# A gated two-layer block: feed-forward products kept in PSUM, high parts moved to ScalarE, the down projection one expert behind

## The chip, the cores and the metric

One core of one Trainium2 chip runs the whole program as one launch. The metric is the device time in microseconds; for the kernel before, three runs gave 1088.89, 1092.85 and 1094.4 us, with a median of 1092.85 us.

## The reference, cut to what matters

The input x is 8 sequences of 256 tokens with 256 features (2048 tokens). Two layers follow each other. Each layer adds a cross-attention over 77 context rows, scaled by tanh of a gate, and then adds a feed-forward, scaled by tanh of another gate.

The first feed-forward has 8 experts of width 704, and the expert is chosen by position:

```
x = inputs.reshape(B, E, C, D)           # E = 8, C = 32 tokens of each sequence
gate = einsum('becd,edf->becf', x, w1)
up   = einsum('becd,edf->becf', x, w3)
h    = silu(gate) * up
out  = einsum('becf,efd->becd', h, w2)
```

So each expert sees 8 x 32 = 256 tokens. The second feed-forward has one shared expert of width 1024 for all 2048 tokens, and 7 routed experts of width 1024. Each token goes to its two best routed experts, and each routed expert has 732 slots.

## The kernel before, in words

**Two parts for each number.** All feed-forward products are made from pairs: a high part (the value written in the type fp32r) and a low part (the value less its high part). One product takes three matmuls (`mm3`, L241 to L243): high by high, one high by low, one low by high. The weights come from HBM as fp32 pieces of 128 x 512 (256 KB) into `raw`. ScalarE copies a piece to `w_hi` (`split13` L768 for the gate and up pieces, `split2` L772 for the down pieces), and GpSimd subtracts it to get `w_lo` (L1496).

**First feed-forward** (`first_layer` on each engine, 8 experts). An expert has six gate and up tiles of 128 hidden rows; tile 0 has gate and up rows of the last 64 hidden units side by side, the others have gate in the left half and up in the right half of one PSUM bank of 512. TensorE does 6 matmuls for tile 0 and 12 for each other tile, 66 in all, and then 36 matmuls of the down projection into the two banks `bank_p`. Tile m goes to bank `2 + m % 3`, one of three, so TensorE waits until VectorE has made the product of tile m - 3. ScalarE makes `silu` (L927) and splits the next expert's pieces behind it. VectorE makes the product (L1214) from `silu` and the up half in PSUM into `prod` in SBUF, casts it to `first_hid_hi` (L1218), and subtracts to get `first_hid_lo` (L1222). It also subtracts two of the three down pieces (L1246), since GpSimd has seven others to do. After the sixth tile TensorE goes straight on to the down projection of the same expert, and for each hidden tile it waits for VectorE's low part. Then ScalarE (L940) and VectorE (L1251) each do four scalings of 32 rows out of `bank_p` into `yh`, and these release the next expert's down projection. SyncE (L341 to L349) loads the pieces in one queue, in this order: down piece, gate and up piece, each with a wait for the low part whose place it takes.

**Second feed-forward.** The shared expert runs in four chunks of 512 tokens. Chunk 0 is interleaved with the end of the second attention and with the routing; chunk 1 follows while GpSimd scatters the rows to the slots in HBM with 32 indirect DMAs (L1632). Then come the 7 routed experts, each with two halves of 366 slots and 8 tiles a half (12 matmuls of 366 columns a tile), then six down projections of 122 slots. Chunks 2 and 3 of the shared expert are last, beside 32 indirect gathers on GpSimd (L1647). Here too VectorE does product, cast and subtraction of every tile (`hidden`), ScalarE does silu and the splits, and GpSimd the weights' low part. The first half of a routed expert (8 tiles) carries four down pieces of its own expert; the second half carries the eight gate and up pieces of the next.

**What sets the order.** It is all written by hand: each engine's program is a list, and counting semaphores order them. `gu_psum` says that a tile is in PSUM, `silu_done`, `gu_free` (product made), `hid_hi_done` and `hid_ready` follow it.

Of the kernel before, what the change touches and what calls it, by code (L numbers as in the profile page):

```python
# [48 lines left out]
def flamingo_program(nc, x, ctx_t, attn_w, rows, cols, gates, router_w, w_first, w_second, xe, ye, v_d, out):  # L49
    with ExitStack() as scope:  # L50
# [50 lines left out]
        v_rows = sb("v_rows", [P, 2, D])  # L101
        kb = sb("kb", [P, 2, KT, SC])
        prob_t = sb("prob_t", [P, KT * PT, S])
# [6 lines left out]
        prod = sb("prod", [P, 2, PIECE])  # L110
        first_hid = place[0]
        first_hid_hi = sb("first_hid_hi", [P, M0, S], F32R)
        first_hid_lo = sb("first_hid_lo", [P, M0, S], F32R)
        assert place[0] == first_ffn_end
        place[0] = first_hid
# [91 lines left out]
        y0_psum, y0_done, y0_first = sem("y0_psum"), sem("y0_done"), sem("y0_first")  # L207
# [23 lines left out]
        GU_SHARED = M0 * E0  # L231
# [32 lines left out]
        def _(sp):  # L264
# [85 lines left out]

            for m in range(M0):
                gate_up_load(1, m)
            with sp.Fori(0, E0 - 2) as e:
                for m in range(M0):
                    if m < 3:
                        down_load(e + 1, m)
                    gate_up_load(e + 2, m)
            for j in range(3):
                down_load(E0 - 1, j)

            for m in range(M0):
                sp.wait_ge(lo13, M0 * (E0 - 1) + m + 1)
                sp.dma_start(raw[:, m, :], w_second[0, m]).then_inc(raw_in[m], 16)

# [70 lines left out]
        def _(pe):  # L435
# [180 lines left out]
            def first_layer(e):  # L616

                for m in range(M0):
                    pe.wait_ge(hi13, M0 * e + m + 1)
                    pe.wait_ge(lo13, M0 * e + m + 1)  # L620
                    pe.wait_ge(gu_free, M0 * e + m + 1)
                    for gu in range(1 if m == 0 else 2):
                        for kt in range(KT):
                            c = kt * (P if m == 0 else 2 * P) + gu * P
                            rhs = [a[:, kt, :].rearrange("p (b s) -> p b s", s=S)[:, :, bass.ds(e * C0, C0)] for a in (act_hi, act_lo)]
                            last = mm3(banks[2 + m % 3][:, gu * S:(gu + 1) * S], w_hi[:, m, c:c + P], w_lo[:, m, c:c + P],
                                       rhs[0], rhs[1], kt == 0, kt == KT - 1)
                    last.then_inc(gu_psum, 1)
                pe.wait_ge(y0_done, 2 * e + 2)
                for k in range(M0):  # L630
                    j, c = k // 2, k % 2 * D
                    pe.wait_ge(hid_ready, hid_count(M0 * e + k))
# [6 lines left out]
                    for h in range(HALVES):  # L639
                        last = mm3(bank_p[h][:, 0:D], first_hid_hi[:, k, h * P:(h + 1) * P], first_hid_lo[:, k, h * P:(h + 1) * P],  # L640
                                   w_hi[:, M0 + j, c:c + D], w_lo[:, M0 + j, c:c + D], k == 0, k == M0 - 1)
                last.then_inc(y0_psum, 1)

# [88 lines left out]
            with pe.Fori(0, E0) as e:  # L732
                first_layer(e)
# [30 lines left out]
        def _(act):  # L764
# [164 lines left out]
            def first_layer(e, i, part):  # L929

                for m in range(M0):
                    src = banks[2 + m % 3]
                    silu_of(M0 * e + m, m % 2, src[0:64, 0:S] if m == 0 else src[:, 0:S], 64 if m == 0 else P, S)
                    if m < 3:
                        split2(M0 + m, e + 1, M0 + m)
                    split13(m, e + 2, m)

                act.wait_ge(y0_psum, e + 1)
                for j in range(B // HALVES):
                    last = nc.scalar.activation(  # L940
                        yh[i * C0:(i + 1) * C0, j, bass.ds(part * D, D)], bank_p[0][j * C0:(j + 1) * C0, 0:D],
# [777 lines left out]
```

## Time and profile before

| what | value |
|---|---|
| median of three runs | 1092.85 us (1088.89 to 1094.4) |
| profiled execution, first to last instruction (the span) | 1084.2 us |
| its own whole time | not given apart from the three runs; the median lies 8.65 us above the span |
| TensorE matmul busy | 927.4 us (86%) |
| VectorE busy | 768.7 us (71%) |
| GpSimd busy | 517.0 us (48%) |
| ScalarE busy | 368.4 us (34%) |

The profile names the engines PE (TensorE matmul), PEld (its weight load), DVE (VectorE), ACT (ScalarE), POOL (GpSimd) and SP (SyncE). A number such as L1222 is the line of the kernel. PEclk is the granted clock of TensorE as a share of full speed. Matmuls are pipelined, so a matmul's own duration is longer than the distance from its start to the next start; the distance is what it costs. Work outside the span is what the launch adds before the first instruction and behind the last.

### The profile page before, as it was taken

The numbers are of one execution on the slowest core, as the hardware profiler recorded it, in microseconds if no ns is written. First come the engines' busy times: TensorE is split into PE (matmuls) and PEld (weight loads), VectorE is DVE, ScalarE is ACT, GpSimd is POOL, SyncE is SP. The second block draws the span as 40 slices with busy tenths as digits, with TensorE's granted clock in tenths as the row PEclk, the third lists the DMA queues.
The fourth block names the chain that finished last, engine by engine and source line by source line (L and its number), as shares of the span: only waits on it lengthen the run. The fifth ranks groups of instructions, "written<-read, shape, count | busy, mean of one in ns | idle before, by whom it ended". The sixth has DMA issues, their size and how long they took to land.

```text
span 1084.2 us, 17578 instructions
## 1 busy us (share of the span) xinstructions
PE 927.4 (86%) x5464; PEld 815.0 (75%) x5464; DVE 768.7 (71%) x1375; ACT 368.4 (34%) x773; POOL 517.0 (48%) x479
## 2 busy tenths in 40 slices
PE   5888887787876879888773999999999999999758
PEld 3666666787874657666562789999999999998637
DVE  4899995978785899998731666758494949475237
ACT  2454453454442444445210232323241414132001
POOL 5667664646362866664567223223142424131740
PEclk9999999988886999999996899999999999999859
DMA  5321112443431000001211232314141413040321
GB/s 181 123 66 38 61 32 85 129 132 126 135 116 31 16 11 10 10 12 43 78 64 59 65 102 65 122 57 135 40 141 36 135 42 129 21 124 29 93 82 59
DMA packets 74860, 82.27 MB, mean 76 GB/s; under 512 B 33902, under 2 KB 47666, under 8 KB 74692
## 3 DMA queue, kind: packets, MB, share of 16 engines
q1 hardware_dynamic: 71748, 74.30, 22.0%
q0 software_dynamic: 3072, 7.46, 2.3%
q8 instruction: 21, 0.34, 0.1%
q14 instruction: 19, 0.16, 0.0%
HBM read 64.57 MB, written 18.10 MB: 76 GB/s over the span
## 4 chain that ended last, share of the span: by engine, by line
PE 47%; DVE 24%; issue 15%; another core or an unknown queue 4%; ACT 4%; POOL 3%; DMA 2%; DVEq 1%; ACTq 0%; SPq 0%; POOLq 0%
PE score L241 9%; PE score L242 8%; PE score L243 8%; PE bank_p L241 5%; DVE total L1084 5%; PE bank_p L243 5%; PE bank_p L242 5%; DVE xn L1039 4%; DVE mx L1075 4%; DVE stats L1014 2%; DVE prob L1079 2%; DMA raw<-w_second_d 2%; DVE prod L1214 1%; PE bank L496 1%
## 5 line engine op out<-in xcount | busy, mean ns | idle before, releaser
L1496 POOL TENSOR_TENSOR w_lo<-raw,w_hi 128x512 fp32r<-128x512 f32 x158 | 211.5, 1350 | 342.8 <-ACT w_hi L772 223.1
L927 ACT ACTIVATE silu<-score 128x366 f32<-128x366 f32 (+3 forms) x192 | 90.8, 473 | 426.3 <-PE score L243 315.8
L1214 DVE TENSOR_TENSOR prod<-silu,score 128x366 f32<-128x366 f32 (+3 forms) x192 | 101.1, 527 | 81.3 <-ACT silu L927 65.3
L241 PE MATMUL score<-xe_hi,w_hi 128*128 128x366 f32 x448 | 149.6, 334 | 2.3 <-DVE prod L1214 2.0
L242 PE MATMUL score<-xe_lo,w_hi 128*128 128x366 f32 x448 | 148.4, 331 | 0.0
L243 PE MATMUL score<-xe_hi,w_lo 128*128 128x366 f32 x448 | 147.1, 328 | 0.0
L241 PE MATMUL score<-act_hi,w_hi 128*128 (+1 forms) x304 | 109.0, 358 | 35.4 <-issue 22.9
L241 PE MATMUL bank_p<-w_hi,hid_hi 128*122 128x256 f32 (+1 forms) x464 | 131.6, 284 | 4.0 <-issue 2.0
L243 PE MATMUL bank_p<-w_hi,hid_lo 128*122 128x256 f32 (+1 forms) x464 | 130.4, 281 | 2.3 <-issue 2.3
L242 PE MATMUL bank_p<-w_lo,hid_hi 128*122 128x256 f32 (+1 forms) x464 | 130.3, 281 | 1.2 <-issue 1.2
L1486 POOL TENSOR_TENSOR prob<-prob,recip 128x616 f32<-128x616 f32 x64 | 96.6, 1511 | 66.0 <-DVE recip L1086 65.9
L1218 DVE CAST hid_hi<-prod 128x366 fp32r<-128x366 f32 (+1 forms) x144 | 116.0, 806 | 5.0
L243 PE MATMUL score<-act_hi,w_lo 128*128 (+1 forms) x304 | 105.5, 347 | 4.2 <-issue 4.1
L242 PE MATMUL score<-act_lo,w_hi 128*128 (+1 forms) x304 | 106.4, 350 | 2.7 <-issue 2.5
L241 PEld LDWEIGHTS score<-act_hi,w_hi 128*128 128x128 f32 x304 | 62.2, 205 | 47.7 <-issue 30.3
L241 PEld LDWEIGHTS score<-xe_hi,w_hi 128*128 128x128 f32 x448 | 84.4, 188 | 6.3 <-DVE prod L1214 4.8
L241 PEld LDWEIGHTS bank_p<-w_hi,hid_hi 128*122 128x122 f32 (+1 forms) x464 | 85.5, 184 | 4.7 <-DVE hid_lo L1222 1.9
L243 PEld LDWEIGHTS bank_p<-w_hi,hid_lo 128*122 128x122 f32 (+1 forms) x464 | 85.9, 185 | 3.9 <-issue 3.9
L807 ACT ACTIVATE prob<-prob 128x616 f32<-128x616 f32 x64 | 46.0, 718 | 123.1 <-DVE prob L1079 123.0
L1222 DVE TENSOR_TENSOR hid_lo<-prod,hid_hi 128x366 fp32r<-128x366 f32 (+1 forms) x136 | 84.2, 619 | 4.7
L477 PE MATMUL score<-kb,q_t 128*128 (+2 forms) x256 | 84.0, 454 | 3.2 <-ACT q_t L801 2.9
L242 PEld LDWEIGHTS bank_p<-w_lo,hid_hi 128*122 128x122 f32 (+1 forms) x464 | 85.7, 185 | 1.0 <-issue 0.8
(141 smaller groups left out, 1941.6 us busy)
## 6 DMA issues: line engine op xcount, KB each, us to landing
raw<-w_second_d SPq DMA_DIRECT2D x108, 256.0 KB, 5.8
raw<-w_first_d SPq DMA_DIRECT2D x72, 256.0 KB, 3.1
slots_in<-yh SPq DMA_DIRECT2D x8, 640.5 KB, 3.1
yh<-slots_in SPq DMA_DIRECT2D x7, 732.0 KB
slots_out<-yh SPq DMA_DIRECT2D x7, 732.0 KB
v_blk<-values SPq DMA_DIRECT2D x256, 5.0 KB, 1.9
wa<-attn_w_d SPq DMA_DIRECT2D x8, 256.0 KB, 5.1
residual<-x_d SPq DMA_DIRECT2D x1, 1792.0 KB, 9.7
```

The costliest lines, as they stand in the source:

```text
L241: nc.tensor.matmul(o, a_hi, b_hi, start=start, stop=False)
L242: nc.tensor.matmul(o, a_hi, b_lo, start=False, stop=False)
L243: return nc.tensor.matmul(o, a_lo, b_hi, start=False, stop=stop)
L477: last = nc.tensor.matmul(score[u % 2][:, c:c + w], q_t[:, dt, qt * P:(qt + 1) * P], kb[:, b % 2, dt, c:c + w], start=True, stop=True)
L807: nc.scalar.activation(pv, pv, ACT.Exp).then_inc(exp_done, 1)
L927: nc.scalar.activation(silu[0:rows_n, buf, 0:width], src, ACT.Silu).then_inc(silu_done, 1)
L1084: nc.vector.tensor_reduce(total[:, u], of_heads(prob[u]), AX_X, ALU.add).then_inc(sum_done, 1)
L1214: nc.vector.tensor_tensor(prod[0:rows_n, buf, 0:width], silu[0:rows_n, buf, 0:width], up, ALU.mult).then_inc(gu_free, 1)
L1218: nc.vector.tensor_copy(hi, prod[0:rows_n, buf, 0:hi.shape[-1]]).then_inc(hid_hi_done, 1)
L1222: nc.vector.tensor_tensor(lo, prod[0:rows_n, buf, 0:hi.shape[-1]], hi.bitcast(F32), ALU.subtract).then_inc(hid_ready, 1)
L1486: nc.gpsimd.tensor_tensor(by_row(prob[u]), by_row(prob[u]), recip[:, u].unsqueeze(1).to_broadcast([P, KV, HT]), ALU.mult).then_inc(norm_do ...
L1496: return nc.gpsimd.tensor_tensor(w_lo[:, at, :], raw[:, slot_f, :], w_hi[:, at, :].bitcast(F32), ALU.subtract)
```

## The change

- **First feed-forward, hidden tiles.** Each of the six tiles has its own PSUM bank (0 to 5). VectorE writes the product over the up half in PSUM. ScalarE copies it from there to the high part, and VectorE subtracts the high part from the product in PSUM to get the low part.
- **First feed-forward, order.** High and low parts have two buffers (even and odd experts), and the down weights too. TensorE does the gate and up tiles 0 and 1 of expert e, then the down projection of expert e - 1, then tiles 2 to 5 of expert e. After the last expert its own down projection follows.
- **First feed-forward, outputs.** ScalarE and VectorE each scale one bank of 128 rows at once into `y0_rows`, and SyncE moves them to `yh` with four DMAs for an expert. The last expert's outputs go as before. The loops of ScalarE and VectorE are partly written out.
- **Routed experts and shared chunks 1 to 3.** ScalarE makes the high part of the hidden tile, one tile behind its silu. VectorE makes the product of tile f and then the low part of tile f - 1, and it also makes the weights' low parts, which leave GpSimd's list.

```diff
             def first_gate_up(e, m):
+                pe.wait_ge(hi13, M0 * e + m + 1)
+                pe.wait_ge(lo13, M0 * e + m + 1)
+                pe.wait_ge(hid0_ready, M0 * e + m + 1)
...
+                            last = mm3(banks[m][:, gu * S:(gu + 1) * S], w_hi[:, m, c:c + P], w_lo[:, m, c:c + P],
+            def first_down(e, par):
+                pe.wait_ge(y0_kept, 2 * e + 2)
...
+                    pe.wait_ge(hid0_ready, M0 * (e + 1) + k + 1)
...
+            def first_layer(e, par, before_it):
+                for m in range(M0):
+                    first_gate_up(e, m)
+                    if m == 1 and before_it:
+                        first_down(e - 1, 1 - par)
# ScalarE
+                for m in range(M0):
+                    first_silu(e, m)
+                    if m > 0:
+                        first_high(e, par, m - 1)
                     if m < 3:
+                        split2(M0 + m, e + 1, M0 + 3 * par + m)
                     split13(m, e + 2, m)
+                    if m == 1 and before_it:
+                        act.wait_ge(y0_psum, e)
...
+                        nc.scalar.activation(y0_rows[:, 1 - par, 0, :], bank_p[0][:, 0:D], ACT.Identity,
+                                             scale=tanh_gate[:, 2:3]).then_inc(y0_kept, 1)
+                first_high(e, par, M0 - 1)
# VectorE
+                nc.vector.tensor_tensor(up, silu0[0:rows_n, m % 4, :], up, ALU.mult).then_inc(prod0_done, 1)
...
+                nc.vector.tensor_tensor(hid0_lo[par][0:rows_n, m, :], up, hid0_hi[par][0:rows_n, m, :].bitcast(F32),
+                                        ALU.subtract).then_inc(hid0_ready, 1)
# SyncE
+            def place_outputs(e):
+                part, i = divmod(e, P // C0)
+                sp.wait_ge(y0_kept, 2 * e + 4)
+                for j in range(P // C0):
+                    sp.dma_start(yh[i * C0:(i + 1) * C0, j::P // C0, part * D:(part + 1) * D],
+                                 y0_rows[j * C0:(j + 1) * C0, e % 2, :, :]).then_inc(y0_moved, 16)
...
                 for m in range(M0):
                     if m < 3:
                         down_load(e + 1, m)
                     gate_up_load(e + 2, m)
+                    if m == 3 and e > 0:
+                        place_outputs(e - 1)
# routed experts, ScalarE
+                        silu_of(n, f % 2, banks[2 + 2 * (f % 2)][:, 0:HC], P, HC)
+                        if hf > 0 or f > 0:
+                            g = (f - 1) % FT
+                            hidden_high(n - 1, g, HC * (hf if f > 0 else 0), HC)
# routed experts, VectorE
-                        hidden(GU_ROUTED + 2 * FT * e + FT * hf + f, f % 2, banks[2 + 2 * (f % 2) + 1][:, 0:HC], P, hf * HC, f, HC)
+                        product(n, f % 2, banks[2 + 2 * (f % 2) + 1][:, 0:HC], P, HC)
+                        if hf > 0 or f > 0:
+                            g, at = (f - 1) % FT, HC * (hf if f > 0 else 0)
+                            hidden_low(n - 1, g % 2, P, hid_hi[:, g, at:at + HC], hid_lo[:, g, at:at + HC])
+                            routed_low(e, hf if f > 0 else 0, g)
# routed experts, GpSimd
-            for f in range(FT):
-                low13(PIECES0 + FT + f, f, f)
-            with pool.Fori(0, E1) as e:
-                expert(e)
-            for j in range(4):
-                low2(3 * E0 + 4 * (STREAM - 1) + j, j, FT + j)
```

## Rows read from the trace of the kernel before

**Rows 1.** Busy time by stage: us, then PE, PEld, DVE, ACT, POOL, PEclk, DMA share.

```profile
184.00:332.00 148.00, 119.49 (x820) 114.80 (x820) 115.13 (x190) 67.38 (x150) 79.26 (x58) 0.86 0.39 121
545.00:597.00 52.00, 27.19 (x148) 23.19 (x148) 11.33 (x28) 6.05 (x9) 36.94 (x36) 0.77 0.18 65
627.00:985.00 358.00, 355.75 (x2428) 351.30 (x2428) 240.44 (x404) 106.43 (x222) 110.20 (x84) 1.00 0.27 87
```

**Rows 2.** Waits, 184 to 332 us: who waited for whom, us, times, longest.

```profile
PE bank_p L241 <- DVE first_hid_lo L1222: 27.8, 16, 2.5
SPq L349 <- DVE w_lo L1246: 45.1, 14, 5.6
```

**Rows 3.** TensorE in order of time: start, duration, [idle before].

```profile
193.67 0.28 PE L241 MATMUL bank_p<-w_hi,first_hid_hi 128*128 128x256 f32 x1
...
228.65 0.29 PE L241 MATMUL bank_p<-w_hi,first_hid_hi 128*128 128x256 f32 x1
...
229.96 0.28 PE L243 MATMUL bank_p<-w_hi,first_hid_lo 128*128 128x256 f32 x1
232.30 0.38 PE L241 MATMUL bank_p<-w_hi,first_hid_hi 128*128 128x256 f32 x1 [2.07 <-DVE first_hid_lo L1222]
...
331.20 0.59 PE L519 MATMUL bank<-wa,ctx_b 128*77 128x256 f32 x2
```

**Rows 4.** Groups by shape, 184 to 332 us: busy us, mean ns, idle before.

```profile
L1496 POOL TENSOR_TENSOR w_lo<-raw,w_hi 128x512 fp32r<-128x512 f32 x56 | 78.0, 1420 | 62.9 <-ACT w_hi L772 59.2 <-ACT w_hi L768 3.6
L1218 DVE CAST first_hid_hi<-prod 128x256 fp32r<-128x256 f32 x40 | 28.8, 720 | 0.0
L1222 DVE TENSOR_TENSOR first_hid_lo<-prod,first_hid_hi 128x256 fp32r<-128x256 f32 x40 | 28.8, 720 | 0.3
L1246 DVE TENSOR_TENSOR w_lo<-raw,w_hi 128x512 fp32r<-128x512 f32 x16 | 27.2, 1698 | 0.0
L1214 DVE TENSOR_TENSOR prod<-silu,score 128x256 f32<-128x256 f32 x40 | 16.4, 409 | 6.4 <-ACT silu L927 6.4
L927 ACT ACTIVATE silu<-score 128x256 f32<-128x256 f32 x40 | 15.1, 376 | 24.7 <-DVE prod L1214 22.7 <-PE score L243 2.0
L768 ACT ACTIVATE w_hi<-raw 128x512 fp32r<-128x512 f32 x48 | 30.0, 624 | 0.0
L1251 DVE TENSOR_SCALAR yh<-bank_p,tanh_gate 32x256 f32 x29 | 13.9, 480 | 20.8 <-PE bank_p L243 20.5
```

**Rows 5.** VectorE in order of time: one operation twice in one expert.

```profile
230.92 1.15 DVE L1222 TENSOR_TENSOR first_hid_lo<-prod,first_hid_hi 128x256 fp32r<-128x256 f32 x1
...
234.22 0.41 DVE L1222 TENSOR_TENSOR first_hid_lo<-prod,first_hid_hi 128x256 fp32r<-128x256 f32 x1
```

**Rows 6.** DMA, 184 to 332 us: GB/s in 40 slices of 3.7 us; issues with KB and us to landing.

```profile
GB/s 0 88 56 143 255 103 144 19 189 275 13 141 3 182 295 19 142 24 153 308 11 139 11 154 315 19 100 42 157 297 42 71 11 103 302 337 27 0 14 149
...
raw<-w_first_d SPq DMA_DIRECT2D x57, 256.0 KB, 2.7
```

**Rows 7.** Groups by shape, 627 to 985 us (routed experts).

```profile
L1218 DVE CAST hid_hi<-prod 128x366 fp32r<-128x366 f32 x112 | 91.8, 820 | 3.9
L1222 DVE TENSOR_TENSOR hid_lo<-prod,hid_hi 128x366 fp32r<-128x366 f32 x112 | 66.6, 595 | 3.9
L1214 DVE TENSOR_TENSOR prod<-silu,score 128x366 f32<-128x366 f32 x112 | 59.5, 531 | 28.7 <-ACT silu L927 28.4
L927 ACT ACTIVATE silu<-score 128x366 f32<-128x366 f32 x112 | 53.5, 478 | 231.7 <-PE score L243 231.7
```

**Rows 8.** ScalarE in order of time, routed experts: one silu to the next.

```profile
641.66 0.48 ACT L927 ACTIVATE silu<-score 128x366 f32<-128x366 f32 x1 [1.54 <-PE score L243]
643.68 0.48 ACT L927 ACTIVATE silu<-score 128x366 f32<-128x366 f32 x1 [1.54 <-PE score L243]
```

**Rows 9.** VectorE, 569 to 571 us (128 x 512, GpSimd on indirect DMAs).

```profile
570.21 0.69 DVE L1222 TENSOR_TENSOR hid_lo<-prod,hid_hi 128x512 fp32r<-128x512 f32 x1
```

**Rows 10.** Waits of the whole trace.

```profile
ACT silu L927 <- remote: 87.6, 4, 41.7
```

More of the change, by code:

```diff
@@ L984, in _ @@
             act.wait_ge(zero_out, 16 * B)
-            per = E0 // HALVES
-            with act.Fori(0, HALVES) as part:
-                for i in range(per):
-                    first_layer(per * part + i, i, part)
+            first_layer(0, 0, False)
+            first_layer(1, 1, True)
+            first_layer(2, 0, True)
+            with act.Fori(1, E0 // 2 - 1) as pair:
+                first_layer(2 * pair + 1, 1, True)
+                first_layer(2 * pair + 2, 0, True)
+            first_layer(E0 - 1, 1, True)
+            last_outputs()
             attention(1)
@@ L1238, in first_layer @@
-                    src = banks[2 + m % 3]
-                    product(n, buf, src[64:P, 0:S] if m == 0 else src[:, S:2 * S], rows_n, S)
+                    first_product(e, m)
                     if m > 0:
-                        hidden_low(*tile(m - 1), first_hid_lo[0:64 if m == 1 else P, m - 1, :])
-                    hidden_high(n, buf, rows_n, hi)
+                        first_low(e, par, m - 1)
+                    if m == 1 and before_it:
+                        dve.wait_ge(y0_psum, e)
+                        if not (isinstance(e, int) and e < 3):
+                            dve.wait_ge(y0_moved, 64 * (e - 2))
+                        nc.vector.tensor_scalar(y0_rows[:, 1 - par, 1, :], bank_p[1][:, 0:D], tanh_gate[:, 2:3], None,
+                                                ALU.mult).then_inc(y0_kept, 1)
@@ L1377, in _ @@
             dve.wait_ge(k_psum, 2)
[L1378 removed]
+            for t in hid0_hi + hid0_lo:
                 last = nc.vector.memset(t[64:P, 0, :].bitcast(F32), 0.0)
@@ L1384, in _ @@
             dve.sem_inc(hid_ready, HID_FREE)
-            dve.sem_inc(y0_done, 2)
-            per = E0 // HALVES
-            with dve.Fori(0, HALVES) as part:
-                for i in range(per):
-                    first_layer(per * part + i, i, part)
+            dve.sem_inc(prod0_done, 4)
+            dve.sem_inc(hid0_ready, M0)
+            dve.sem_inc(y0_kept, 2)
+            first_layer(0, 0, False)
+            first_layer(1, 1, True)
+            first_layer(2, 0, True)
+            with dve.Fori(1, E0 // 2 - 1) as pair:
+                first_layer(2 * pair + 1, 1, True)
+                first_layer(2 * pair + 2, 0, True)
+            first_layer(E0 - 1, 1, True)
+            last_outputs()
             attention(1)
```

174 lines of the change are left out of this document (109 added, 65 removed).

## The prediction, as it was put on record before the changed kernel ran

> **What bounds the kernel now.** I read the table of busy time by stage first. In the routed experts (627 to 985 us) TensorE's matmuls are busy 355.75 of 358.00 us at a granted clock of 1.00: nothing but fewer matmuls helps there. In the first feed-forward (184 to 332 us) they are busy 119.49 of 148.00 us at a clock of 0.86, VectorE 115.13 us and GpSimd 79.26 us [rows 1]. So this stage has room, and the waits say what ends last in it: TensorE's down projection waited 27.8 us in 16 waits for VectorE's low part of the hidden tile [rows 2]. In order of time, the down projection runs the first 12 matmuls at once (two hidden tiles) and then stands still until 232.30, 2.07 us, for a low part [rows 3].
>
> The rest of the stage's loss is the clock. Of the 12 matmuls ahead of that stop the first starts at 228.65 and the last at 229.96, so at full clock they are 1.31 / 11 = 0.119 us apart. From 193.67, the first down projection, to 331.20, when the stage has ended, TensorE issues 8 x 36 + 7 x 66 = 750 matmuls in 137.5 us, 0.183 us each [rows 3]. The waits explain some 28 us, or 0.037 of the 0.064 us more; most of the rest is matmuls behind the waits at a clock below full (mean 0.86 [rows 1], so a mix of 2.4 and 1.2 GHz). Both go if TensorE never waits.
>
> Why VectorE is late: product 0.409, cast 0.720 and low part 0.720 us a tile, six times, and 1.698 us twice for the down weights [rows 4], 14.5 us an expert with the outputs. The cast and the low part are not slow in themselves. The low part takes 1.15 us while GpSimd works and 0.41 us in the same expert when it doesn't [rows 5]. The product, which reads one operand from PSUM, has a mean of 0.409 us [rows 4] beside the same GpSimd.
>
> **The change part by part: first feed-forward.** TensorE's work stays 102 matmuls an expert, 102 x 0.119 = 12.1 us at full clock [rows 3]. The question is whether the others fit below 12.1 us and whether anything is due earlier than they deliver it.
>
> VectorE: six products at 0.41, six low parts, two down weights at 1.70 [rows 4], one output of 128 x 256 at 0.48 (the row of the 32 x 256 output, same columns [rows 4]). The new low part reads the product in PSUM and the high part in SBUF, the same sources as the product: I take 0.41. The upper bound is the low part beside GpSimd, 1.15 us [rows 5]. The product now writes to PSUM, which no row shows; below it can hardly be under the 0.41 of now, above I bound it by the same 1.15. Sum: 2.5 + 2.5 + 3.4 + 0.5 = 8.9 us; with slow low parts 13.3 us; with both slow 17.7 us.
>
> The Trainium skill (SBUF — State Buffer, "SBUF: two separate sides") says that VectorE and GpSimd share one port pair as an exclusive lock, which a VectorE instruction takes when it has two SBUF inputs (against a GpSimd operation that reads SBUF) or runs in a two-port mode. By that rule the low part with its PSUM input never takes the lock and the sum is 8.9 us; the two down weights keep it. The trace agrees as far as it goes: 1.15 against 0.41 us for two SBUF inputs, 0.409 on average for one.
>
> ScalarE: six silus at 0.376, six high parts (bounded by 0.376 below, by the 0.624 of a 128 x 512 copy above; I take 0.376), nine splits at 0.624 and one output at 0.48 [rows 4]: 10.6 us, 12.1 us at the upper bound. It is in order and now waits at tile 1 for the down projection of the expert before. TensorE's order gives 0.7 us for tile 0, 1.4 for tile 1, then 4.2 for the down projection: at 6.3 us ScalarE is released, and silu 2 is due at 7.8. From there it has to do tiles 2 to 5 and then tiles 0 and 1 of the next expert before the next release at 18.4: six silus, six high parts, nine splits, 10.1 us, due at 17.9. It fits by 0.5 us. If it doesn't, what is late is a scaling of `bank_p`, and that is not due for TensorE before the next down projection, a whole turn of slack less its own 6 us. VectorE behind the same release needs 8.9 of its 10.6 us.
>
> GpSimd: seven weights at 1.42 us [rows 4], 9.9 of 12.1 us. Its lows are for the next expert. Tile 5's is split at about 13 us and subtracted by 15 us; TensorE wants it at 22.
>
> Down projection, now 2.1 us of gate and up work later: the last low part follows the end of tile 5 by silu 0.38, product 0.41, a split that stands in ScalarE's queue 0.62, high 0.38, low 0.41, 2.2 us. TensorE is at hidden tile 5 of the down projection only 2.1 + 5 x 0.7 = 5.6 us after the end of tile 5. The wait for a free bank, too, is an expert old with six banks. So nothing is late next, and I expect the 16 waits to be gone.
>
> SyncE and the DMAs: the pieces are 9 x 256 KB and the moved outputs 4 x 64 KB, 2.6 MB an expert, 217 GB/s at 12.1 us. The stage's slices reach 308 and 337 GB/s for 3.7 us [rows 6], and a piece lands in 2.7 us [rows 6], while each load has most of a turn before its split. SyncE's queue now waits 45.1 us for VectorE's down weights [rows 2], and the gate and up loads stand behind it; in the new order these come at 10 and 12 us of the turn and the splits that need the loads behind them at 21 us and later. The four moves an expert stand behind the load of tile 3, and their own condition is older than that load's. I cost them at nothing; if the transfers ran at the 120 to 180 GB/s that surround the peaks [rows 6] the stage would be theirs (see the rivals).
>
> Sum: the first 66 matmuls stay as they are, to 193.67. Then 750 x 0.119 = 89.3 us instead of 137.5: 48.2 us less. I give back 1.5 us for the first turns of longer loops and the last down projection, whose last low parts are due at 3.5 us and come at 2.2 to 3. That leaves 46.7 us. The end of the stage (the last outputs in eight scalings) is as before.
>
> **Routed experts and shared chunks.** A tile is 2.02 us of TensorE (silu to silu, 641.66 to 643.68 [rows 8]). VectorE in the second half: product 0.53, low part 0.54 to 0.60 [rows 7], gate and up weights 0.69 by the row of the same shape with two SBUF inputs [rows 9], together 1.8 us; before it was 0.53 + 0.82 + 0.60 [rows 7]. The upper bound for the weights' low part is 1.70 [rows 4], a row beside a working GpSimd; here GpSimd is idle, so I take 0.69. ScalarE: silu 0.48, high part at most 0.62, split 0.62: 1.7 us. The product of tile f stands behind the low parts of tile f - 1 but TensorE wants it only before tile f + 2. Everything stays below 2.02 us, and as TensorE is never idle now, the gain is 0. In the chunks TensorE sets the pace too. Where the down projection waits for hidden tiles, the new chain is at most 1 us shorter or longer. The two stretches with indirect DMAs hold 87.6 us in which ScalarE's silu waits for a signal that the profile can't attribute, the longest 41.7 us [rows 10]; during the scatter TensorE is busy 27.19 of 52.00 us [rows 1]. The transfers and the work in these stretches stay, so I cost them at 0.
>
> The span comes to 1084.2 - 46.7 = 1037.5 us, and the median, 8.65 us above the span for the kernel before, to 1046.2 us.
>
> **The rivals.**
> - *VectorE stays the bound in the first feed-forward* (0.10). The low part, or the product written to PSUM, takes longer than 0.41. At 13.3 us an expert and with waits that pull the clock down, 14 us: 8 x 14 = 112 us instead of 100 us (9.3 + 89.3 + 1.5), 1058 us. Against it is the mean of 0.409 beside a busy GpSimd.
> - *The transfers become the bound* (0.05). At 180 GB/s an expert takes 14.5 us, 8 x 14.5 = 116 us: 1062 us. Against it: the pauses between the peaks are SyncE's waits, not slow packets [rows 2, 6].
> - *The indirect stretches change* (0.08). Signals from TensorE come late there, for a reason that I can't see. With other neighbours in time, fewer may be late: up to 25 us of TensorE's 52.00 - 27.19 us idle could go, 1020 us. The other direction, 10 us more, is 1055 us.
> - *The routed experts become VectorE's: slower than before* (0.04). The place is the second half, tile by tile. The gain is used up when each of 8 x 7 = 56 tiles costs 46.7 / 56 = 0.83 us more, that is at 2.85 us of VectorE a tile. With weights at 1.70 and a low part at 1.15 a tile is 0.53 + 1.15 + 1.70 = 3.4 us, 1.36 us over TensorE's 2.02: 56 x 1.36 = 76 us, 1122 us. For it: such durations are in the trace. Against it: only beside a working GpSimd, and GpSimd has left this stage.
> - *It doesn't do what it says* (0.03). A wait that I missed ties the down projection to its own expert again, for instance ScalarE's stop at tile 1 delaying the splits; about half the gain is left, 1070 us.
>
> **How the numbers follow.** The forecast has 0.70, with its own range of 1039 to 1055 us (the product or low part up to 0.2 us more at no cost, ScalarE's 0.5 us of margin gone at up to 1 us an expert). The predicted time is 1046 us. The range that leaves out no more than 0.2 goes from 1034 to 1064 us: it leaves out the slower case, the half gain and most of the indirect gain. 0.5% of 1092.85 is 5.5 us, about what a measurement of this kernel can tell from no change. Faster by more: 0.92; within it: 0.03; slower by more: 0.05.
>
> **What would show it.** The down projection's waits for low parts gone, matmul starts 0.119 us apart and PEclk near 1.00 through the stage, its length 99 to 102 us. VectorE's low part and product at 0.41 us beside a working GpSimd; the down weights still at 1.7. The routed stage at 358 us, VectorE's weights at 0.69. The prediction is wrong if the stage is over 107 us, if the routed stage grows by more than 5 us, or if the stretches of indirect DMAs change by more than 5 us.

## The result, and the profile after

Four runs each on one chip: 1040.87 us median (1039.39 to 1041.57) after, 1090.87 us median (1086.1 to 1094.4) before; the ratio is 0.9546, 95% interval 0.952 to 0.9572. The prediction was 1046 us. The profiled execution of the changed kernel has a span of 1037.6 us; the sum of the prediction was 1037.5 us.

The sections between six points in the two traces. All but the last, the end of the span, are starts of TensorE instructions: the first gate and up matmul of the first feed-forward, the first matmul of the second attention (the last row of [rows 3]), the second matmul of the position sums of the routing, the first matmul on slots, and the first matmul of shared chunk 2.

```
                      start   first FF  attention 2  scatter  routed   tail     span
before                184.3     146.9      214.6       81.1    357.6    99.7   1084.2
after                 188.5     100.3      213.4       79.4    353.0   103.0   1037.6
difference             +4.2     -46.5       -1.2       -1.7     -4.6    +3.3    -46.5
predicted                0      -46.7          0          0        0       0    -46.7
```

Busy time of the changed kernel in the first feed-forward, in the middle of it, and in the routed experts, in the columns of [rows 1]: length, PE, PEld, DVE, ACT, POOL, PEclk, DMA share, GB/s.

```profile
188.00:289.00 101.00, 97.58 (x817) 97.43 (x818) 55.36 (x126) 73.23 (x180) 75.07 (x58) 1.00 0.65 196
200.00:284.00 84.00, 84.00 (x707) 84.00 (x706) 45.35 (x104) 59.95 (x150) 63.34 (x49) 1.00 0.67 206
582.00:934.00 352.00, 351.39 (x2419) 350.74 (x2418) 189.44 (x375) 150.71 (x334) 0.00 (x0) 1.00 0.28 89
```

Against the first line of [rows 1], TensorE is busy 97.58 of 101.00 us at a clock of 1.00, where it was 119.49 of 148.00 at 0.86. Its busy time fell too, though it does the same matmuls: they no longer run partly at half clock. VectorE is down from 115.13 to 55.36 us. Between 192 and 286 us the list of waits has no row for TensorE at all, so the first row of [rows 2] is gone. The second is still there and only shorter, 31.6 us where it was 45.1, and TensorE waits for nothing behind it:

```profile
SPq L357 <- DVE w_lo L1348: 31.6, 14, 4.4
```

TensorE in order of time. The first matmul below is the 67th of the stage, the last but one is the 816th:

```profile
196.39 0.28 PE L249 MATMUL bank<-act_hi,w_hi 128*128 x1
...
285.69 0.28 PE L251 MATMUL bank_p<-w_hi,hid_lo_odd 128*128 128x256 f32 x1
288.86 0.41 PE L539 MATMUL bank<-wa,ctx_b 128*77 128x256 f32 x1 [2.89 <-DMA ctx_b<-ctx_d]
```

From 196.39 to 285.69 is 89.3 us for the 750 matmuls that took 137.5 us before [rows 3]. Then TensorE stands 2.89 us for a load of the second attention.

VectorE and ScalarE by shape in the stage: busy us, mean ns, idle before.

```profile
L1322 DVE TENSOR_TENSOR score<-silu,score 128x256 f32<-128x256 f32 x32 | 13.6, 425 | 13.7 <-ACT silu L969 13.7
L1348 DVE TENSOR_TENSOR w_lo<-raw,w_hi 128x512 fp32r<-128x512 f32 x16 | 13.5, 841 | 0.0
L1329 DVE TENSOR_TENSOR hid_lo_odd<-score,hid_hi_odd 128x256 fp32r<-128x256 f32 x16 | 6.7, 418 | 1.2 <-ACT hid_hi_odd L975 1.2
L1342 DVE TENSOR_SCALAR y_rows<-bank_p,tanh_gate 128x256 f32<-128x256 f32 x7 | 3.4, 484 | 15.4 <-PE bank_p L251 10.1 <-DMA yh<-y_rows 5.3
...
L802 ACT ACTIVATE w_hi<-raw 128x512 fp32r<-128x512 f32 x48 | 30.5, 635 | 3.9 <-DMA raw<-w_second_d 3.9
L975 ACT ACTIVATE hid_hi_odd<-score 128x256 fp32r<-128x256 f32 x16 | 6.2, 390 | 0.0
```

The low part, 0.720 us in the mean before [rows 4], takes 0.418 us; the product written to PSUM takes 0.425 us; the down weights' low part fell from 1.698 [rows 4] to 0.841 us, though nothing was done to it. VectorE now waits for ScalarE's silu, that is, for work to arrive.

### The profile page after: what moved, and what is told of

Read it like the earlier page. It is cut to its first block, busy times and chain, and to the rows that moved or that the text cites. A ratio compares the mean times of both kernels' runs of the same rounds, so it can differ in the third digit from the quotient of the medians.

```text
span 1037.6 us, 17237 instructions
## 1 busy us (share of the span) xinstructions
PE 905.1 (87%) x5464; PEld 803.0 (77%) x5464; DVE 642.2 (62%) x1268; ACT 428.9 (41%) x936; POOL 387.0 (37%) x383
## 4 chain that ended last, share of the span: by engine, by line
PE 58%; DVE 23%; issue 11%; POOL 3%; ACT 2%; DMA 2%; DVEq 1%; SPq 0%; POOLq 0%; ACTq 0%
PE score L249 11%; PE score L250 11%; PE score L251 10%; PE bank_p L249 6%; PE bank_p L251 6%; PE bank_p L250 6%; DVE total L1161 5%; DVE xn L1116 5%; DVE mx L1152 4%; DVE stats L1091 2%; DVE prob L1156 2%; DMA raw<-w_second_d 1%; PE score L471 1%; PE bank L516 1%; PE bank L532 1%
## 5 line engine op out<-in xcount | busy, mean ns | idle before, releaser
L961 ACT ACTIVATE silu<-score 128x366 f32<-128x366 f32 (+1 forms) x144 | 72.6, 504 | 342.4 <-PE score L251 296.8
L1292 DVE TENSOR_TENSOR prod<-silu,score 128x366 f32<-128x366 f32 (+1 forms) x144 | 82.0, 569 | 141.7 <-ACT silu L961 132.1
L1759 POOL DMA_INDIRECT act_hi<-slots_out,slot_get x8 | 8.1, 1007 | 406.9 <-DMA slots_out<-yh 404.8
L249 PE MATMUL score<-act_hi,w_hi 128*128 128x512 f32 (+2 forms) x256 | 90.1, 352 | 27.7 <-issue 26.5
L249 PEld LDWEIGHTS bank_p<-w_hi,hid_hi 128*122 128x122 f32 (+1 forms) x464 | 86.5, 186 | 16.8 <-issue 14.3
L1620 POOL TENSOR_TENSOR w_lo<-raw,w_hi 128x512 fp32r<-128x512 f32 x62 | 82.1, 1357 | 22.7 <-ACT w_hi L802 20.9
L250 PE MATMUL score<-act_lo,w_hi 128*128 128x512 f32 (+2 forms) x256 | 88.8, 347 | 0.0
L251 PE MATMUL score<-act_hi,w_lo 128*128 128x512 f32 (+2 forms) x256 | 88.6, 346 | 0.0
L250 PEld LDWEIGHTS score<-xe_lo,w_hi 128*128 128x128 f32 x448 | 84.4, 188 | 0.0
L251 PEld LDWEIGHTS score<-xe_hi,w_lo 128*128 128x128 f32 x448 | 84.2, 188 | 0.0
```

Of the source, the lines that this page charges most:

```text
L249: nc.tensor.matmul(o, a_hi, b_hi, start=start, stop=False)
L250: nc.tensor.matmul(o, a_hi, b_lo, start=False, stop=False)
L251: return nc.tensor.matmul(o, a_lo, b_hi, start=False, stop=stop)
L961: nc.scalar.activation(silu[0:rows_n, buf, 0:width], src, ACT.Silu).then_inc(silu_done, 1)
L1292: nc.vector.tensor_tensor(prod[0:rows_n, buf, 0:width], silu[0:rows_n, buf, 0:width], up, ALU.mult).then_inc(gu_free, 1)
L1620: return nc.gpsimd.tensor_tensor(w_lo[:, at, :], raw[:, slot_f, :], w_hi[:, at, :].bitcast(F32), ALU.subtract)
```

## The experiments

There were twelve runs of eleven kernels, each beside the kernel before on the same chip. They ran on four chips, and on two of these the kernel before takes 1055.5 and 1056.8 us, not 1090. The first feed-forward doesn't differ between the chips: with the changed kernel's code in it, it took 100.1, 100.3 and 103.8 us on the slower ones and 101.1 and 101.2 us on the others (the stretches at fault come below). So for it I compare stage lengths, which are in each trace, and the time of a turn: from one expert's down projection to the next, a mean over the first six turns. The turn is the sharper measure. It was 12.16 us in all five of these runs, while their first matmul came anywhere from 185.5 to 188.5 us and the length moved with it, so a difference of less than 4 us in the length says little.

```
kernel                 turn    first FF   median     before on    ratio [95% interval]
                       us      us         us         that chip
kernel before          18.1    146.9
old_work_no_defer      16.5    136.7      1043.03    1055.49      0.9876 [0.9845, 0.9907]
old_tile_work          15.3    126.3      1069.88    1089.81      0.9806 [0.9779, 0.9833]
psum_only              14.3    112.9      1021.43    1056.84      0.9678 [0.9651, 0.9706]
no_defer               12.1    102.1      1041.87    1089.81      0.9551 [0.9519, 0.9583]
high_dve               12.2    101.6      1003.21    1055.49      0.9513 [0.9482, 0.9544]
prod_sbuf              12.2    100.9      1012.61    1055.49      0.9587 [0.9549, 0.9626]
changed kernel         12.2    100.3      1040.87    1090.87      0.9546 [0.952, 0.9572]
old_tile_short_pool    12.2    100.1      1003.89    1056.84      0.951 [0.9476, 0.9545]
```

The last row has two executions, and its kernel leaves out part of the work (below).

**Which half of the change is it? First the first feed-forward alone.** Routed experts and chunks as before:

```diff
-                            hidden_high(n - 1, g, HC * (hf if f > 0 else 0), HC)   # ScalarE
+                        hidden_high(n, f % 2, P, hid_hi[:, f, hf * HC:(hf + 1) * HC])   # VectorE
+            with pool.Fori(0, E1) as e:
+                expert(e)   # the weights' low parts on GpSimd
```

> The new first feed-forward with the routed experts and shared chunks as before (VectorE makes product, high and low part, GpSimd the weights' low parts). Theory: nearly the whole gain is the first feed-forward's. The two traces give -49.7 us for that stage and +4.2 us ahead of it, and the routed stage gives -4.6 us by itself; so this kernel should stand 4 to 6 us above the changed one, a span of 1042 to 1044 us, with the routed stage back at 357.6 us. Rival: the 4.6 us of the routed stage are a matter of where code and data came to lie, not of who makes the high part; then the span is within 1.5 us of 1037.6.

1044.6 us (1043.01 to 1048.05) against 1089.81, ratio 0.9587 [0.9557, 0.9617]; span 1041.3 us. That is 3.7 us above the changed kernel, just short of the theory's 4 to 6 and far from the rival's 1.5, but the 3.7 us don't lie where the theory put them: the routed stage is 356.0 us (3.0 more than changed), not 357.6, the scatter stretch 82.7 us (3.3 more), and the tail 100.4 us (2.5 less). The -49.7 us of the expectation count the first feed-forward to its last down projection, without the 3.2 us behind it.

**Then the routed part alone.** The reverse edit on the kernel before.

> The first feed-forward as before, the routed experts and shared chunks as changed. Theory: 4.6 us less than the kernel before in the routed stage (357.6 to 353.0 us) and nothing elsewhere, a span of 1079 to 1081 us. Rival one: the routed part gains nothing by itself (my prediction, 0), a span of 1084. Rival two: the 3.2 us more that the changed kernel's tail takes (99.8 to 102.9 us from the third shared chunk to the end) come from this part; then this kernel shows them as well and is near 1083 us.

1087.9 us (ten runs) against 1089.81, ratio 0.9979 [0.9957, 1.0001]; span 1085.4 us. Routed stage 353.1 us, 4.5 less than before, as the theory said; tail 103.1 us, 3.4 more, as the second rival said. In all the routed part gives 1.9 us by the medians, and the interval reaches 1, so by itself it can't be told from nothing. The span is 4 us over the theory's 1079 to 1081 us. Its trace shows one more thing: it reaches the first feed-forward at 187.5 us with the same code for which the profiled run of before needed 184.3, 3.2 us less.

**Is the delay of the down projection needed?**

```diff
                 for m in range(M0):
                     first_gate_up(e, m)
-                    if m == 1 and before_it:
-                        first_down(e - 1, 1 - par)
+                first_down(e, par)
```

> The changed kernel with one thing undone, on TensorE alone: the down projection of expert e stands right behind its own tile 5 again, not behind tile 1 of the next expert. Theory by the prediction's steps: the low part of tile 5 is ready 2.2 to 3 us after the tile, TensorE wants it at 3.5 us, so the delay by one expert is not what removes the waits; 0 to 2 us more in the stage. Rival: the low part comes after 3.5 us, TensorE stops once an expert for 1 to 2 us, and the clock falls with it: 10 to 20 us more.

1041.87 us median on a chip where before took 1089.81, and a span of 1037.1 us; a turn is 12.1 us. Its four executions took 1038.9, 1040.66, 1043.08 and 2703.28 us. The median is that of all four, the ratio leaves the last one out, and why it took so long is open. It isn't needed: with the new tile work the low part of tile 5 is there when TensorE asks for it, and the trace has no wait of TensorE for it. The 1.8 us more in the stage lie ahead of its first down projection and behind its last, not in its turns.

**Is it the order, or the work on the tile?** The changed order, banks and outputs, with the tile work of before:

```diff
-                nc.vector.tensor_tensor(up, silu0[0:rows_n, m % 4, :], up, ALU.mult).then_inc(prod0_done, 1)
+                nc.vector.tensor_tensor(prod0[0:rows_n, m % 4, :], silu0[0:rows_n, m % 4, :], up, ALU.mult).then_inc(prod0_done, 1)
+                nc.vector.tensor_copy(hid0_hi[par][0:rows_n, m, :], prod0[0:rows_n, m % 4, :]).then_inc(hid0_high, 1)
```

> The changed order, banks and output moves, but the tile work as before: VectorE makes product into SBUF, high and low part from SBUF. Theory: VectorE's work sets the stage, 6 x (0.41 + 0.72 + 0.72) + 2 x 1.70 + 0.5 = 15.0 us an expert against TensorE's 12.1; the stage is 17 to 25 us longer than with the changed tile work, a span of 1055 to 1063 us. Rival: the order alone (the down projection an expert behind) removes the waits and VectorE's durations shrink when nothing waits; then less than 5 us more.

The stage took 126.3 us, 26 more than changed, just over the expected 17 to 25, and the span 1067.7 us, over the expected 1055 to 1063; the whole took 1069.88 us in the median, ratio 0.9806. VectorE sets the pace. By shape, from 187 to 314 us:

```profile
L1337 DVE TENSOR_TENSOR hid_lo_even<-prod,hid_hi_even 128x256 fp32r<-128x256 f32 x20 | 20.4, 1018 | 0.1
L1357 DVE TENSOR_TENSOR w_lo<-raw,w_hi 128x512 fp32r<-128x512 f32 x16 | 19.6, 1228 | 0.0
L1330 DVE CAST hid_hi_odd<-prod 128x256 fp32r<-128x256 f32 x20 | 14.3, 717 | 0.0
```

The low part takes 1.0 us. And the waits of TensorE and the stretch in the middle of the stage, with the columns as above:

```profile
PE bank_p L250 <- DVE hid_lo_odd L1337: 10.0, 8, 2.6
PE bank_p L250 <- DVE hid_lo_even L1337: 6.3, 7, 1.6
...
200.00:305.00 105.00, 92.11 (x706) 89.22 (x704) 92.64 (x145) 51.59 (x112) 69.19 (x48) 0.95 0.53 165
```

VectorE is busy 92.64 of 105 us, 13.5 us of a turn of 15.3, and TensorE waits twice an expert for its low part (15 waits).

**The same without the delay.** Both edits together:

> The tile work of before on VectorE (product into SBUF, high and low part from SBUF) and the down projection right behind its own tile 5; what is left of the change in the first feed-forward is a bank for each of the six tiles, two buffers for the hidden parts and the down weights, and the outputs scaled 128 rows at once and moved by DMA. Theory: with VectorE as the bound, the delay by one expert does matter: TensorE stops for the last low parts and VectorE then for TensorE; 8 to 14 us longer than the 126.3 us with the delay. Rival: VectorE alone sets the pace in both orders, within 3 us of 126.3; then the banks and the outputs alone are the 20 us between 126.3 and the 146.9 us of before.

136.7 us, 10.4 more than with the delay, as the theory said (8 to 14). So the delay is worth 10 us where VectorE is the bound and nothing where it isn't: the two halves of the change don't add. What this kernel still has of the change in the stage, six banks, double buffers and the outputs in whole rows, is worth the other 10.2 us up to the 146.9 of before.

**Who makes the high part?** VectorE again, but from PSUM:

```diff
+                nc.vector.tensor_copy(hid0_hi[par][0:rows_n, m, :], up).then_inc(hid0_high, 1)
-                nc.scalar.activation(hid0_hi[par][0:64 if m == 0 else P, m, :], up, ACT.Copy).then_inc(hid0_high, 1)
```

> The changed kernel, but in the first feed-forward VectorE makes the high part of the hidden tile, copying the product out of PSUM; product and low part stay in PSUM. Theory: what costs is not the copy but an operation with both operands in SBUF beside GpSimd; the copy from PSUM takes about 0.4 us, VectorE needs 6 x (0.43 + 0.40 + 0.42) + 2 x 0.84 + 0.48 = 9.7 us an expert, under TensorE's 12.2, and the stage stays within 2 us of 100.3. Rival: taking the high part off VectorE is what made room; the copy costs the 0.72 us of before and TensorE waits again, 5 to 12 us more.

```profile
200.00:284.00 84.00, 84.00 (x707) 84.00 (x706) 57.17 (x144) 48.20 (x106) 66.02 (x48) 1.00 0.66 203
...
L1326 DVE CAST hid_hi_odd<-score 128x256 fp32r<-128x256 f32 x16 | 6.6, 411 | 0.0
L1333 DVE TENSOR_TENSOR hid_lo_odd<-score,hid_hi_odd 128x256 fp32r<-128x256 f32 x16 | 6.7, 417 | 0.1
```

TensorE is busy all 84 us, VectorE 57.17; the copy from PSUM takes 0.411 us where the copy from SBUF took 0.72. The stage is 101.6 us. ScalarE's help isn't needed either. (The stage lengths 101.6 and 100.3 us can't be told apart; the turns are the same.)

**Where does the product lie?** In SBUF again, ScalarE still makes the high part:

```diff
-                up = banks[m][64:P, 0:S] if m == 0 else banks[m][:, S:2 * S]
+                up = prod0[0:rows_n, m % 4, :]   # high (ScalarE) and low (VectorE) part
```

> The changed kernel, but in the first feed-forward the product goes into SBUF and the high and low part are made from there; ScalarE still makes the high part. Theory: the low part takes 0.7 to 1.0 us again (two operands in SBUF beside GpSimd) and the down weights up to 1.7; VectorE needs 6 x (0.42 + 1.0) + 2 x 1.7 + 0.48 = 12.4 us an expert, just over TensorE's 12.2: the stage is 2 to 8 us longer. Rival: the place of the operand does not matter (low part 0.42 us), no change.

```profile
200.00:284.00 84.00, 83.83 (x704) 83.65 (x703) 64.94 (x104) 63.42 (x152) 66.17 (x48) 1.00 0.65 207
...
L1334 DVE TENSOR_TENSOR hid_lo_even<-prod,hid_hi_even 128x256 fp32r<-128x256 f32 x20 | 18.1, 918 | 0.0
L1353 DVE TENSOR_TENSOR w_lo<-raw,w_hi 128x512 fp32r<-128x512 f32 x16 | 19.7, 1230 | 0.0
```

The durations came as expected (0.9 and 1.23 us), the time of the stage did not: 100.9 us. VectorE is busy 64.94 of 84 us, 9.4 us a turn and not the 12.4 of the theory, which had put the low part at 1.0 and the down weights at 1.7 us. So VectorE was still under TensorE's 12.2. TensorE waits for a low part only in the last down projection, twice, 2.5 us together. Outside this stage the run is 4 us longer in the second attention and 2.8 in the tail than the kernel with the high part on VectorE; why stays open.

**Is GpSimd the cause of the long durations?** The tile work of before, with GpSimd's low parts of the gate and up weights cut short. The kernel leaves out the other 508 of 512 columns of six pieces an expert, so it only serves to see the durations:

```diff
-                    low13(M0 * (e + 1) + m, m, m)
+                    short_low(m, m).then_inc(lo13, 1)   # 4 of 512 columns
```

> The tile work of before on VectorE in the changed order (the stage took 126.3 us), with six of the seven weights' low parts that GpSimd makes for an expert cut to 4 columns of 512; so the low parts of those weights are left out. Theory: the long durations of VectorE's SBUF operations come from GpSimd working beside them; with GpSimd nearly idle the low part takes 0.42 us or less, the high part 0.4, and the stage comes to within 3 us of 100.3. Rival: the durations belong to the operations (1.0 us and 0.7 us stay) and the stage stays at 126.

```profile
L1357 DVE TENSOR_TENSOR w_lo<-raw,w_hi 128x512 fp32r<-128x512 f32 x16 | 10.9, 683 | 0.0
L1337 DVE TENSOR_TENSOR hid_lo_odd<-prod,hid_hi_odd 128x256 fp32r<-128x256 f32 x20 | 8.4, 421 | 0.1
L1330 DVE CAST hid_hi_even<-prod 128x256 fp32r<-128x256 f32 x20 | 5.7, 286 | 0.0
```

It is. The same instructions on the same operands: low part 1.0 to 0.42 us, copy 0.7 to 0.29 us, down weights 1.23 to 0.68 us, and the stage 126.3 to 100.1 us. With GpSimd out of the way, nothing of the new tile work was needed.

**The smallest edit.** The kernel before, only the product left in PSUM:

```diff
+                    if m >= 3:
+                        pe.wait_ge(hid_ready, hid_count(M0 * e + m - 3))
...
-                    product(n, buf, src[64:P, 0:S] if m == 0 else src[:, S:2 * S], rows_n, S)
+                    nc.vector.tensor_tensor(up_of(m), silu[0:rows_n, buf, 0:S], up_of(m), ALU.mult).then_inc(gu_free, 1)
```

> The kernel before with one thing changed in the first feed-forward: VectorE writes the product over the up half in PSUM and makes high and low part from there (TensorE waits for the low part, not the product, before it reuses a bank). Banks, order, outputs, ScalarE and GpSimd as before. Theory: the place of the operand is nearly the whole change; VectorE needs 6 x (0.43 + 0.41 + 0.42) + 2 x 1.2 + 4 x 0.48 = 11.9 us an expert, about TensorE's 12.2, with a wait of 1 to 2 us an expert at the hand-over behind the outputs: the stage takes 104 to 114 us instead of 146.9. Rival: with three banks held longer and the down projection behind its own tiles, TensorE still waits and the clock falls; over 120 us.

The stage took 112.9 us, inside the theory's 104 to 114: 34 of the 46.5 us come from this edit alone, ratio 0.9678. VectorE needs 65.13 of 90 us (196 to 286), 10.3 us of a turn of 14.3, so it is no longer the bound; and the granted clock is 1.00 there, although TensorE is busy only 80.25 of the 90 us. What is left is not the wait that I expected. First TensorE's waits, then ScalarE in order of time:

```profile
PE score L241 <- ACT w_hi L770: 9.8, 7, 1.4
PE score L241 <- DVE first_hid_lo L1245: 1.7, 8, 0.2
...
225.45 0.62 ACT L770 ACTIVATE w_hi<-raw 128x512 fp32r<-128x512 f32 x1
229.46 1.91 ACT L942 ACTIVATE yh<-bank_p,tanh_gate 32x256 f32 x4 [3.39 <-PE bank_p L243]
231.40 0.38 ACT L929 ACTIVATE silu<-score 64x256 f32<-64x256 f32 x1
```

Its four outputs stand in ScalarE's list ahead of the next splits. It waits 3.39 us for the down projection, takes 1.91 us for the outputs, and so the next weights come late. In the changed kernel ScalarE has one output instruction a turn, for the expert before. That this, and not the six banks, gives the last 2.1 us a turn is argued from these rows, not tried by itself.

**Which half of the routed edit?** The weights' low parts to GpSimd again, the high part left on ScalarE:

> The changed kernel, but in the routed experts and shared chunks GpSimd makes the weights' low parts again; ScalarE keeps the high part of the hidden tile. The question is which half of the routed edit gave 357.6 to 353.0 us. Theory: ScalarE's high part; it took 0.82 us a tile off VectorE, whose product was late at the start of an expert and behind the slots' low parts (TensorE waited 2.0 us in two waits, and 0.3 us an expert). VectorE has still less to do here, so the routed stage stays at 353 to 354 us. Rival: GpSimd's absence; with it back VectorE's operations on SBUF get longer and the stage is 356 to 358 us. The times in the indirect stretches depend on the chip and are not part of the question.

Routed stage 353.1 us: the theory holds, ScalarE's high part is what shortens this stage, not GpSimd's absence. By how much is less sure than the 4.5 us: the stage takes 352.9 to 354.4 us in the runs with ScalarE's high part and 356.0, 357.4 and 357.6 us in the three without. The tail is back at 100.5 us. The first feed-forward is 103.8 us long because it starts at 185.5 us, 3.1 us earlier than in the changed kernel, and ends some 0.5 us later. 1040.17 us median against 1089.59, ratio 0.9543 [0.951, 0.9576], the same as the changed kernel.

**Fewer signals in the indirect stretches.** Three gate and up tiles for a signal in chunks 1 and 2:

```diff
+                    at, count = (2, 4, 0)[f % 3], int(f in (2, 5, 7))
...
+                if count:
+                    last.then_inc(gu_psum, 1)
```

> The changed kernel, but in shared chunks 1 and 2 TensorE signals the gate and up tiles in groups of three (three, three, two) over six banks instead of one by one over four, and the four down projections of chunks 0, 1 and 2 with one signal into the two halves of two banks. Same matmuls. Theory: while GpSimd issues indirect DMAs, TensorE's signals arrive one after the other with 10 to 20 us between them; with 5 signals where there were 16 in the first zone, TensorE gets 10 to 25 us of the zone's idle time back (79.4 us from the position sums to the first routed expert), and up to 10 in the second. Rival one: a signal is held until the indirect DMAs are over, however few there are: no change in either zone, or 2 to 4 us more for the coarser hand-over. Rival two: what is late is the end of TensorE's own work, then it is 5 us longer.

> The same kernel as with fewer signals, once more, because the chip of that run showed no late signals at all, in no kernel. Where they are late (the two indirect stretches take 79.4 and 103 us in the changed kernel, not 71.6 and 74.1), the theory of signals that are delivered one by one, some 17 us apart, gives 72 to 75 us for the first stretch and 80 to 95 us for the second. Rival: a late signal waits for the end of the indirect DMAs whatever their number; 79 and 103 us stay, or more. On a chip without late signals it is 72.8 and 76.3 us again and says nothing.

1007.41 us against 1055.49 (0.9545 [0.9518, 0.9573]) and 1007.45 us against 1056.84 (0.9539 [0.9506, 0.9573]), on two chips. Neither chip has the late signals, so the question stays open. The coarser hand-over costs some 1 us in the first stretch there (72.8 and 73.0 us against 71.6 to 72.0 in the others with the changed code). In the second, 76.3 us both times lies among the 74.1 to 76.9 us of the others.

## Why the prediction was right, point by point

- **What bounds the stage: right.** TensorE's 750 matmuls took 89.3 us, to 0.1 us the predicted 750 x 0.119. The 1.5 us given back turned out as 3.2 us behind the last down projection (the load of the context), and the first 66 matmuls, which I left as they were, were 1.5 us quicker (7.9 us for 9.3). That these two cancelled is luck.
- **VectorE: right, one term too large.** Product 0.425 and low part 0.418 us for the 0.41 that I took. The down weights were put at 1.70 us and took 0.84, and that gives 7.2 us a turn, not 8.9. VectorE's busy time, 45.35 in 84.00 us, is 6.6 us a turn, because half of its operations start some 0.08 us before the one ahead has ended. The mean of 0.84 hides two lengths: seven of the 16 operations take 0.68 us with GpSimd idle beside them, and nine take 0.93 to 1.11 us with GpSimd at work; before, 15 of 16 took 1.76 to 1.78 us. The 1.70 was read from those, and the prediction kept it for the new order. GpSimd's operations got a little shorter as well (1.420 [rows 4] to 1.36 us). One sum was wrong without a consequence: the 14.5 us an expert of before are the terms without the outputs; with four at 0.48 they give 16.4, and the busy time was 14.4 (115.13 / 8).
- **ScalarE: right.** The high part took 0.390 us (0.376 taken), and it was never late for TensorE.
- **The rule cited: right.** Beside a working GpSimd two kinds of operation were slow: two SBUF inputs (1.0 against 0.42 us) and the copy from SBUF to SBUF (0.7 against 0.29 us). The product with one operand in PSUM was 0.41 to 0.43 us with GpSimd busy or idle. The Trainium skill (SBUF — State Buffer, "SBUF: two separate sides") says that these two kinds take the port pair that VectorE shares with GpSimd. The trace agrees at each place; that it is this port, and not something else that a working GpSimd does, no run here tells apart.
- **SyncE and the DMAs: right.** Within the turns nothing on TensorE's path waits for them; the stage moves 196 GB/s. Behind the turns TensorE stands 2.89 us for the load of the context, which the prediction didn't have. ScalarE and VectorE each wait twice for the moved outputs, 2.1 to 2.6 us a time, and nobody waits for that.
- **The causes' shares: not asked, and they would have come out wrong.** I treated the change as one. The runs show that three parts overlap: product in PSUM with the high part on VectorE (turn 12.2 us), high part on ScalarE with the product in SBUF (12.2), down projection not delayed (12.1). Each could be left out alone; leaving out the first two together costs 26 us. The stage has a floor, TensorE's 12.1 us a turn, and in the new order any edit that brings VectorE under it is enough. In the old order it isn't: with only the product in PSUM VectorE needs 10.3 us a turn, and the turn is 14.3.
- **Routed experts: 0 predicted, -4.6 us measured.** I read 355.75 busy of 358.00 us [rows 1] as no room. But the busy time is that of overlapping matmuls and hides pauses shorter than one. The first expert had two waits for VectorE's product, 2.0 us together, and in each later one the 36 matmuls behind the slots' transposes took 6.20 us and take 5.92 now. The step that failed is "TensorE is never idle now". The size that the rival of slower routed experts hung on was right: the weights' low part is 0.685 us there (0.69 taken).
- **The indirect stretches: 0 predicted, -1.7 and +3.3 us.** The first is within the spread: 79.4 to 81.5 us in the five kernels with ScalarE's high part there, on chips with late signals. The second has a cause in the change: the tail is 103.0 to 103.2 us in the four kernels with the weights' low parts on VectorE and 99.7, 100.4 and 100.5 us in the three without, on the same chips. On the other chips there is no such difference (74.5 us without, 74.1 to 76.9 with). How these low parts lengthen it wasn't shown.
- **Start: +4.2 us.** Most likely not the change. Up to here the kernels have nearly the same code, and the stage starts between 184.3 and 188.7 us in their profiled runs; the profiled run of before was the quickest. What moves the start is open.
- **The distance from span to median: wrong, 8.65 us.** A run's time is its span plus 1.8 us (1039.39 and 1037.6). By the same 1.8 us the span of before, 1084.2, makes 1086.0 us, which fits the run of 1086.1 us, the quickest of four; the rest of the 8.65 was that place among its fellows. The changed kernel spreads by 2.2 us only. This term is the whole of the 5 us between 1046 and 1040.87; the sum in the span, 1037.5, met 1037.6, but with -4.6, +4.2 and +3.3 us cancelling in it, and -1.7 and -1.2 beside them. To meet it to 0.1 us was luck; the 46.5 us of the first feed-forward were not.

## What to carry to other kernels

Before moving work to another engine, look at how long one instruction takes with its neighbour busy and idle: here some 6.4 of VectorE's 14.4 us an expert were lengthening beside GpSimd (an estimate: six times 0.72 - 0.29 and 0.72 - 0.42, twice 1.70 - 0.68), and leaving the operand in PSUM took most of it away without an instruction more. Work out the floor of the stage (here TensorE's 12.1 us a turn) first: edits that each bring the late engine under the floor don't add, and what they save beyond it is not seen. And take a profiled run's place among its fellows into account before adding a distance from span to median.

## What the runs showed of the hardware that was not expected

**Chips differ by 35 us in the same kernel, and in two stretches only.** On two of the chips TensorE's signals arrive late while GpSimd issues indirect DMAs; on the other two they don't. The rows "<- remote", waits for a signal that the profile can't attribute, are in the traces of before and changed and in all five from the two slower chips, and in none of the seven from the other two. The scatter stretch, first the changed kernel where they are late:

```profile
ACT silu L961 <- remote: 45.6, 3, 22.8
DVE prod L1292 <- ACT silu L961: 29.0, 7, 23.2
PEld score L249 <- issue: 27.3, 2, 19.5
```

Then the kernel with the high part on VectorE, whose code in this stretch is the same, on a chip where they aren't:

```profile
ACT xe_hi L1045 <- PE bank L731: 33.7, 2, 32.7
DVE xe_lo L1394 <- ACT xe_hi L1045: 23.7, 2, 22.7
PEld bank L731 <- DMA yh<-slots_in: 22.1, 1, 22.1
```

There no silu waits for a remote signal; TensorE finishes shared chunk 1 and then waits 22.1 us for the scattered rows to come back, a dependency of the program. The stretch takes 71.6 us for 79.4, the tail 74.1 for 103.0, and every other section is within 2 us of the changed kernel's. The code of before shows the same: in the kernel with only the product in PSUM, whose code in both stretches is that of before, they take 71.3 and 74.5 us for 81.1 and 99.7, together 35 us less, about the whole difference of the medians. In the trace of before, the matmuls of four tiles of shared chunk 1 end near 561, 564, 574 and 592 us, and their signals arrive at 568.4, 585.9, 596.5 and 596.6 us; the other engines' signals are prompt. So the unattributed waits of [rows 10] come with the chip and not with the kernel; what makes them is open. The change gains as much on either kind of chip: the ratios of the kernels whose turn is 12.1 to 12.2 us lie between 0.951 and 0.959.
